# Ternary quantization in a two-layer AdaLN kernel: the scale multiplied by the signs on GpSimd

## The reference

```python
def ternary_quant(w_fp32, g=GROUP_SIZE):
    w = w_fp32.astype(jnp.bfloat16)
    w_g = w.reshape(-1, g)
    scale = jnp.clip(jnp.mean(jnp.abs(w_g), axis=-1, keepdims=True), 1e-08, None)
    q = jnp.clip(jnp.round(w_g / scale), -1, 1)
    w_hat = (q * scale).reshape(w.shape)
    return w + jax.lax.stop_gradient(w_hat - w)
```

## Time and profile before

| | us |
|---|---|
| median of three runs | 1219.66 |
| the profiled execution | 1222.45 |
| its span in the profile | 1220.3 |
| TensorE matmul busy | 1099.1 (90%) |
| VectorE busy | 872.3 (71%) |
| ScalarE busy | 527.3 (43%) |
| GpSimd busy | 169.7 (14%) |

### The profile page before, as it was taken

One profiled execution on the slowest core, in us unless ns is written; L12 is line 12 of the kernel. 1 busy time (PEld: TensorE's weight loads), 2 busy tenths in 40 slices (PEclk: granted clock), 3 DMA queues, 4 the chain that ended last, 5 costly groups with the idle time before them and its releaser, 6 DMA issues. The chain is left out here.

```text
span 1220.3 us, 13140 instructions
## 1 busy us (share of the span) xinstructions
PE 1099.1 (90%) x4432; PEld 543.0 (45%) x4432; DVE 872.3 (71%) x1602; ACT 527.3 (43%) x1102; POOL 169.7 (14%) x143
## 2 busy tenths in 40 slices
PE   7888778669998989998899899999998999999997
PEld 6546633444453434343344344444444444444443
DVE  4787764546675778877868799668898587785654
ACT  3555643235542546436326354244535163431421
POOL 3100000011110322112121131212302000200100
PEclk9756878559998999989999999999999999999999
DMA  8410110403230043213212002113020011020000
GB/s 261 174 56 35 53 35 18 173 4 108 80 121 1 18 141 97 89 58 114 76 53 70 18 27 64 40 35 100 26 68 18 1 53 35 18 70 1 1 35 35
DMA packets 47523, 75.55 MB, mean 62 GB/s; under 512 B 8320, under 2 KB 16000, under 8 KB 47328
## 3 DMA queue, kind: packets, MB, share of 16 engines
q1 hardware_dynamic: 47168, 74.62, 19.0%
q0 software_dynamic: 288, 0.09, 0.2%
HBM read 66.16 MB, written 8.54 MB: 61 GB/s over the span
## 5 line engine op out<-in xcount | busy, mean ns | idle before, releaser
L1482 PE MATMUL g_g<-h,wt 128*128 128x512 f16 x1728 | 400.5, 380 | 7.2 <-DVE hid L1764 3.5
L1482 PEld LDWEIGHTS g_g<-h,wt 128*128 128x128 bf16 (+1 forms) x1728 | 167.1, 98 | 225.1 <-issue 32.4
L1496 PE MATMUL g_d<-wt,parts 128*128 128x512 bf16 (+1 forms) x864 | 206.6, 382 | 5.5 <-DVE tmp L1597 2.7
L2071 ACT ACTIVATE parts<-hid 128x512 f16<-128x512 f32 x108 | 68.0, 629 | 306.7 <-DVE hid L1764 306.7
L1405 PE MATMUL g_o<-shared 128*128 128x512 f32 x384 | 180.3, 613 | 13.6 <-DVE tmp L1576 5.6
L1757 DVE SCALAR_TENSOR_TENSOR hid<-th,g_g 128x512 f32<-128x512 f32 x108 | 73.6, 681 | 137.9 <-ACT th L2064 137.7
L1496 PEld LDWEIGHTS g_d<-wt,parts 128*128 128x128 f16 x864 | 83.5, 99 | 114.9 <-issue 15.2
L2181 POOL TENSOR_TENSOR acc<-acc,sqh 128x512 f32<-128x512 f32 x52 | 77.4, 1488 | 305.8 <-ACT sqh L2077 305.8
L1405 PEld LDWEIGHTS g_o<-shared 128*128 128x128 f32 x384 | 74.0, 196 | 96.2 <-issue 71.1
L1769 DVE TENSOR_TENSOR parts<-hid,parts 128x512 f16<-128x512 f32 x108 | 89.3, 827 | 26.7 <-ACT parts L2071 26.5
L2164 POOL TENSOR_TENSOR g_rstd<-g_var,g_power 128x4 f32<-128x4 f32 x20 | 24.2, 1210 | 341.2 <-DVE g_var L1522 341.2
(11 more groups left out here) (315 smaller groups left out, 1564.5 us busy)
## 6 DMA issues: line engine op xcount, KB each, us to landing
shared<-in_w SPq DMA_DIRECT2D x48, 256.0 KB, 2.7
x<-in_codes SPq DMA_DIRECT2D x32, 264.0 KB, 3.1
w_raw<-in_wt SPq DMA_DIRECT2D x16, 512.0 KB, 3.7
x<-in_wmod SPq DMA_DIRECT2D x7, 1024.0 KB, 5.2
wmod<-in_wmod SPq DMA_DIRECT2D x5, 1024.0 KB, 10.1
codes_f<-x SPq DMA_DIRECT2D x32, 132.0 KB, 1.7
gates<-in_x SPq DMA_DIRECT2D x4, 1024.0 KB, 8.0
x<-in_x SPq DMA_DIRECT2D x4, 1024.0 KB, 6.0
```

Source lines behind the costliest of these rows:

```text
L1482: mm = nc.tensor.matmul(pg[i][:], wide[:, k, o:o + P], h16[f % 2][:, s, k], start=(s == 0 and k == 0), stop=(s == 1 and k == KD - 1))
L1496: mm = nc.tensor.matmul(pd[j][:], parts16[:, t % 3, s, j * P:(j + 1) * P], wd[:, m, :], start=(m == 0 and s == 0), stop=(done and s == 1))
L2071: nc.scalar.activation(parts16[:, t % 3, 0], hid[:, t % 2], ACT.Copy).then_inc(hi_ready, 1)
```

## The change

GpSimd multiplies the signs of a pair by its scales, in place in wsgn (a new function `signed`), once ScalarE has cast the signs and VectorE has filled both halves of the scale (step 1 of the pair). It counts in a new semaphore, w_signed. VectorE's step 3 waits for that and multiplies the comparison by the signed scale; its old step 4 is gone, so a pair has six steps, and the next pair's step 0 now follows step 2. GpSimd's program in head is written in half-steps, so that its power operations and the products stand in the order in which VectorE comes to them. In groups the number of steps that are counted for a pair of w_proj stays five; only its name changes.

```diff
-WSTEPS = 7
+WSTEPS, DOWN_STEPS = 6, 5
...
-    w_cast, mean_full, w_steps = (sem(n) for n in ("w_cast", "mean_full", "w_steps"))
+    w_cast, mean_full, w_steps, w_signed = (sem(n) for n in ("w_cast", "mean_full", "w_steps", "w_signed"))
...
-        return (q + 1, 0) if i == 3 else (q, i + 1 if i < 3 else i)
+        return (q + 1, 0) if i == 2 else (q, i + 1 if i < 2 else i)
...
     @block.gpsimd
     def _(pool):
+        def signed(q):
+            pool.wait_ge(w_cast, 3 * q + 2)
+            pool.wait_ge(w_steps, number[q, 1])
+            nc.gpsimd.tensor_tensor(wsgn[:, q % 2], wsgn[:, q % 2], wscale[:, q % 2], ALU.mult).then_inc(w_signed, 1)
+
...
-        layer_norm_root(1)
-        length_root(0)
-        length_root(1)
-        layer_norm_root(2)
-        layer_norm_root(3)
-        length_root(2)
-        length_root(3)
+        for h in range(FROM, HALVES):
+            for u, i in stages(h):
+                if u and i == 4:
+                    layer_norm_root(u)
+                if i == 19:
+                    length_root(u)
+            for n in share(h, STEPS):
+                if ternary_step(n)[1] == 1:
+                    signed(ternary_step(n)[0])
+
...
             elif i == 3:
-                dve.wait_ge(w_cast, 3 * q + 2)
+                dve.wait_ge(w_signed, q + 1)
                 ins = nc.vector.tensor_tensor(whash[:], whash[:], wsgn[:, q % 2], ALU.mult)
             elif i == 4:
-                ins = nc.vector.tensor_tensor(whash[:], whash[:], scale, ALU.mult)
-            elif i == 5:
                 dve.wait_ge(w_cast, 3 * q + 3)
                 ins = nc.vector.tensor_tensor(whash[:], whash[:], wt, ALU.subtract)
...
-            wt, at = keep["wt"][:, 2 * (PAIRS + p):2 * (PAIRS + p) + 2], TERNARY + (WSTEPS - 2) * p
+            wt, at = keep["wt"][:, 2 * (PAIRS + p):2 * (PAIRS + p) + 2], TERNARY + DOWN_STEPS * p
```

More of the change, by code:

```diff
@@ L1490, in product @@
             if f == 0 and m % 2 == 0:
-                pe.wait_ge(w_steps, TERNARY + (WSTEPS - 2) * (m // 2 + 1))
+                pe.wait_ge(w_steps, TERNARY + DOWN_STEPS * (m // 2 + 1))
             for j in range(NJ):
@@ L2049, in cast @@
             if p and i < 2:
-                act.wait_ge(w_steps, TERNARY + (WSTEPS - 2) * (p - 1) + i + 1)
+                act.wait_ge(w_steps, TERNARY + DOWN_STEPS * (p - 1) + i + 1)
             dst, kind, scale = ((wabs, ACT.Abs, 2.0), (wsgn, ACT.Sign, 1.0),
```

## The result

The changed kernel takes 1227.27 us (median of five runs, 1224.98 to 1227.88) against 1219.66, which is 7.6 us more by the medians. The forecast was +12.1 us. The direction and the mechanism are the forecast's; the size is less than half of it. The measured value lies between the forecast and the rival of a short hold.

What follows compares the result with a forecast made beforehand. VectorE was taken to bound some stretches of the head, TensorE waits others. Holds of 20.0 us less 7.9 saved gave +12.1 us, 1231.8 us from the 1219.66 median; range 1216 to 1244, the forecast's own 1225 to 1241.

Steps and rivals of the forecast that it cites:

- rival of a short hold: Head: a product takes 1.26 us, set by bytes, and holds VectorE 1.07; total 1220 us; chance 0.12.
- What bounds the head: First block: VectorE bounds some stretches, TensorE waits end others; a microsecond won or lost there is one at the end.
- The mechanism: Head: GpSimd reading SBUF holds VectorE operations with two SBUF inputs, for GpSimd's time less 0.2 us, 2.1 per product.
- The unaffected kinds: VectorE operations that read PSUM or only one SBUF tensor are not held beside GpSimd.
- The time of a product: GpSimd's 128x1024 bf16 multiplication in the head: 2.3 us, twice the 512-column f16 row, as columns set the time.
- The walk for each pair: VectorE's program order followed from each of 16 products in the head: holds of 0.2 to 2.1 us, 25.1 in sum.
- What is hidden, and how much of the removal counts: Head: waits hide holds at pairs 2, 11, 12, 14, 15; 12 of 16 removed steps count, 7.9 of 10.6 us.
- The holds: VectorE stalls beside GpSimd's products in the head: 20.0 us remain of 25.1 after hiding.
- The removal: Taking VectorE's 16 scale multiplications out of the head saves 7.9 us.
- What was moved past: GpSimd's roots sharing its queue with products, and ScalarE's signs waiting for an earlier masking: both cost nothing.
- That of no hold: Head: GpSimd always finds a gap, VectorE never stands, and the saved 7.9 us remain: 1211.8 us; chance 0.13.
- The worse case: Head: a product takes 3.0 us, holds 2.8, nothing is hidden: +25, 1244.7 us; chance 0.11.

Runs made afterwards that it cites:

- halved product: The changed kernel with each GpSimd product cut in two of 128x512, the first issued three steps earlier: +3.8 us (0.9 to 6.6) against the kernel before.
- the addition alone: The kernel before, all seven VectorE steps kept, plus 16 GpSimd products into a tile nobody reads: +14.7 us (10.9 to 18.4).
- the products with the old places: The change with VectorE's seven places and order of before, a one-column memset replacing the removed step: +10.1 and +12.3 us against the kernel before.
- the work put back: The changed kernel plus one VectorE 128x1024 bf16 multiplication per pair before the masking, result unread: +17.5 us (13.0 to 21.9) against the kernel before.
- late products: The kernel before plus GpSimd products into an unread tile, only for pairs 11 to 15: +3.5 us (0 to 7.2).
- the removal with the old places: Seven places and order of before, one-column memsets replacing VectorE's scale step and GpSimd's product, scale left out: -3.4 us (-6.5 to -0.4) against before.
- the extra step: The kernel before plus one VectorE 128x1024 bf16 multiplication for each of 16 pairs, into an unread tile: +10.3 us (6.7 to 13.9).

## Why the prediction was right or wrong

**What bounds the head** was right: in both traces of the change the stretch behind it has kept its length (1001.2 and 1002.0 us against 1000.7), and the holds came where the rows put them.

**The mechanism** was right, and both halves of it are shown: the products hold VectorE (+14.7 alone, with VectorE's steps unchanged), and for operations with two SBUF inputs it is their reading (memsets of the same length leave those alone). That the hold is GpSimd's time less 0.2 us also held: 1.93 to 1.95 of 2.12. The unaffected kinds were those of the earlier trace rows: L829, which reads PSUM, and the reductions kept their durations. The prediction was wrong to spare every operation with only one SBUF tensor: the TENSOR_SCALAR steps L757 and L781 were held by 0.42 and 0.22 us in the change, and one by 0.9 us beside a halved product. In the sum of the change this is 0.6 us.

**The time of a product** was taken as 2.3 us, twice the f16 row; it is 2.12. The full hold is then 1.93 and not 2.1. That row was of an operation with f32 inputs; the bf16 one takes 8% less a column.

**The walk for each pair** gave 25.1 us; 20.9 are held. Pairs 1, 3, 5, 6, 7, 10, 11 and 13 held 1.86 to 1.95 where the walk had 2.1 or 1.9; pairs 9 (1.15), 14 (1.03), 0 (0.23) and 2 (0.42) were as walked, within 0.2. Pairs 4 and 15 held nothing where it had 1.0 and 1.2: VectorE waited there for a mask (2.35 and 1.52 us), and the product ran under that wait. Pairs 8 (1.53) and 12 (1.26) held less than 1.9, since VectorE came to the weighting 0.84 and 0.65 us behind the product's start. With the product's time this is 4.2 us of the error.

**What is hidden, and how much of the removal counts**, is the step that failed most. The forecast let 5.1 of the 25.1 us be hidden and 2.7 of the 10.6 saved be lost, which is a net 2.4 us fewer waits. The waits fell by 7.5 (and by 7.5 in the second trace of the change): 5.1 us of the error. With the 4.2, and the 11.0 that the removed instructions had as busy time instead of 10.6, this closes the gap between 12.1 and the profile's 2.4; between the timed 5.5 and the profile's 2.1 lies the spread of single executions.

Both terms were mis-sized when taken alone. The holds were to cost 20.0 us; the addition alone cost 14.7 (10.9 to 18.4) with 23.5 held, so some 9 us were hidden and not 5.1. The removal was to give 7.9; alone it gave 4.4 (2.0 to 7.0) and 3.4 (0.4 to 6.5). Together these make +10.3, and the change measured 5.5 and 5.7, so some 5 us stay unexplained by the parts. A likely reading is that each edit changes what the other is worth, because a product meets other work once a step is gone, but it is not shown: the same 16 steps are priced at 11.8 us beside products in the new order and at 2.4 to 4.6 in the old one.

**What was moved past** cost nothing, as said: the keys' wait for GpSimd's root is 0.2 us in both kernels, and the masking waits for no signs.

**The rivals.** The short hold is refuted by 2.12 us and 1.93 held. Its sum of about +0.2 us was no farther from +5.5 than the forecast's +12.1, but that was luck and not its mechanism. That of no hold is refuted by the groups by line. The worse case needed 3.0 us for a product and nothing hidden; neither was so. Of what the prediction wanted to see, two failed: the head ended at 221.66 and not near 232, and the waits for TensorE fell by a good deal more than a little.

**What stays open.** Why the products with the old places cost 4 to 7 us more than the change. The linked memset (an estimate of 1.9 us) and pair 0's wait for its product (1.4 us) explain up to about 3 us. The new order alone is not it, since with the work put back it costs as much as the old one. The held sums hardly differ (21.6 against 20.9). TensorE's clock is a rival that no run isolates: from 105 to 150 us the granted clock was 0.61 and 0.70 in the two traces with the old places, 0.77 and 0.81 in the two of the change, and the heads ended at 228.17, 224.80, 221.66 and 222.36. Whether the lower clock is a cause of the longer head or follows from it stays open, and the intervals of the two kernels touch, so the difference may be as small as 1 or 2 us.

## What to carry to other kernels

An idle GpSimd is not free for elementwise work that reads SBUF: while it reads, a VectorE operation with two SBUF inputs stands still, and so did some with one (TENSOR_SCALAR), so price such a move by VectorE's next operation of that kind (here 1.93 us per product, paid for 0.69 us saved), not by GpSimd's idle share. Look in the trace of before for places where the two already overlap; the stretched durations (a maximum far above the median of a line) give the price before anything is built. And where two engines take turns as the bound, time the edits together and don't rely on a sum of single ones: the parts here made +10.3 us and the whole +5.5 and +5.7, and the same 16 steps were priced at anything from 2.4 to 11.8 us, with intervals several us wide.

## What the hardware showed that was not expected

The head's length varies from one execution to the next by about as much as the change is worth, and one difference that the traces show is in TensorE's clock. Busy us by stretch (length, PE, PEld, DVE, ACT, POOL, PEclk, DMA, GB/s), first before, then the kernel with late products, which has the same program up to 147 us except for GpSimd's order:

```profile
40.00:50.00 10.00, 10.00 (x42) 8.11 (x42) 8.98 (x24) 7.19 (x13) 0.00 (x0) 0.78 0.74 267
```

```profile
40.00:50.00 10.00, 9.58 (x42) 6.79 (x42) 9.37 (x23) 6.13 (x12) 0.00 (x0) 1.00 0.96 344
```

With the granted clock at 1.00 instead of 0.78 of full speed (2.4 GHz for the whole stretch, against a mixture of both levels) the second kernel was 2.4 us ahead at 63 us, having been 0.3 us ahead at 41, and it ended its head at 217.66, earlier than the kernel before, with 7.5 us of holds in it. TensorE had been at full clock in both until 30 us and was at half clock, 0.50, in both from 60 to 70 us. The DMA engines moved more in that stretch as well (344 against 267 GB/s), so the clock is not shown to be the only cause.

The stretch behind the head varies too, though none of the edits touches it. From the last state update to the end it took 1000.5 to 1002.1 us in eleven of the fourteen traces, 998.2 with the late products, 1006.7 in the removal with the old places and 1007.4 with the extra step. Busy us by stretch, with the columns as above (PEclk is the third number from the end), first before, then the removal with the old places:

```profile
370.00:380.00 10.00, 7.61 (x27) 2.27 (x26) 5.45 (x9) 1.95 (x8) 0.00 (x0) 1.00 0.01 2
380.00:390.00 10.00, 7.87 (x22) 3.27 (x22) 7.09 (x16) 1.84 (x10) 1.26 (x1) 0.66 0.00 0
```

```profile
370.00:380.00 10.00, 7.01 (x22) 2.16 (x21) 6.82 (x13) 1.15 (x2) 1.26 (x1) 0.82 0.00 0
380.00:390.00 10.00, 10.00 (x27) 4.58 (x26) 1.42 (x5) 1.36 (x10) 0.00 (x0) 0.50 0.00 0
```

The half clock lasted longer there in the second, and most of its 6.0 us are lost around this place (3.2 us, and 1.0 some 70 us later). So a part of a timed difference of 5 or 10 us can lie where the edit changed nothing. One profile of each kernel can't rank two kernels that differ by 5 us; the repeated timing can, and the durations of single operations can.
